# A hybrid attention, expert and recurrent block on one Trainium2 core: input and output laid out by channels, the last residual split between two engines, and blank matmuls moved around the first two expert inputs

## The chip, the cores and the metric

The program runs on one core of a Trainium2 chip. The metric is device time in microseconds (us): 404.32 for the kernel before, the median of 3 runs (403.74 to 404.45). TensorE is called PE here (its weight loads PEld), VectorE DVE, ScalarE ACT, GpSimd POOL and SyncE SP. SP and ACT issue the transfers.

## The reference, cut to what matters

Two images of 16 x 16 positions with 64 channels go through a chain of residual blocks: windowed attention with a gate, a norm, full attention, dilated attention over tokens, a mixture of 8 experts, a causal attention, and a recurrence over the 256 tokens. The last two residuals and the end read:

```python
t = t + _L2_ffn_ref(_ln_t(t), ...)        # gate, top 2 of 8 experts, GELU between two products
t = t + _L3_attn_ref(_ln_t(t), ...)
t = t + _L3_ffn_ref(_ln_t(t), ...)        # the recurrence
...
def step(carry, xs):                       # once for each of 256 tokens
    h, c = carry
    i_t = jax.nn.sigmoid(xi_t + h @ V_i)
    g_t = jnp.tanh(xg_t + h @ V_c)
    o_t = jax.nn.sigmoid(xo_t + h @ V_o)
    c_new = h * c + i_t * g_t
    h_new = o_t * jnp.tanh(c_new)
    return ((h_new, c_new), h_new)
```

A step needs the `h` and `c` of the step before, so the 256 steps run one after the other.

## The kernel before

Everything is held on chip with the two images times 64 channels on the 128 partitions and the 256 tokens along the free axis. Each engine has its own list of instructions, written out by hand in program order; semaphores (`on("name")`) link them, and an engine waits in order. Nothing reorders the work.

**The start.** SP loads `x` token by token (`xtm`, L209: 128 tokens on the partitions, 64 channels in a row, so pieces of 256 bytes), then the constants `cst` and the rest. ACT issues the first weights `w0s` and the vectors `vcs`. PE runs 9 blank matmuls (`keep_clock`, L417, operands zero) and then turns `xtm` into `xf` (channels on the partitions) with two transposes (L425) and one more blank; DVE copies the result out (L783). Then come the products with the weights for keys (L430), queries (L431) and the gate (L432), and DVE makes the masked keys `km` (L792), which the first scores (L459) wait for. DVE takes the smallest score of a row at L813, which also reads the position table `rel`.

**The experts.** After the third norm, PE makes the gate's logits (L643), then `up(0)` and `up(1)`, the first products of two experts (L652), then 8 blank matmuls, then `up(2)`, which first waits for the GELU of expert 0 on ACT (L370) and has one blank matmul of its own. DVE works out the experts' weights meanwhile. From `up(2)` on, PE goes through `up`, `down` (L668) and the spreading of weights (L661) without a gap. ACT makes one `exp` for the gate, changes its function table and then runs the GELUs in order. POOL adds the experts' results (`t3part`, L256).

**The recurrence.** A loop over 16 bodies of 16 steps (PE L748, ACT, DVE L1031, each with its own copy). In a step PE adds the products with the two parts of h, `ha` and `hb` (L740), ACT makes the gates (L394, L396, L400) and the tanh (L406), and DVE makes `ha` (L1039), `hb` (L1042), the cell (L1045), `hs` (L1047) and `hc` (L1049). SP and POOL have nothing to do in it.

**The end.** When `hs` is complete, DVE adds `t4` in two halves (L1052), PE turns each half back to tokens (L769), DVE copies each out of PSUM (L1055), and SP stores each with a transfer of its own (L218).

Of the kernel before, what the change touches and what calls it, by code (L numbers as in the profile page):

```python
# [33 lines left out]
UP_FIRST = 5  # L34
PADT = 3
CHUNK = 8
STEPS_IN_BODY = 2 * CHUNK
HSCALE = 256.0
VSCALE = 16.0
# [35 lines left out]
def build(nc, x, const, later, vec, positions, w0, w1, w2, w3, w4, w5, out):  # L75
    with ExitStack() as ctx:
        def sb(name, shape, dt=F32):
            return ctx.enter_context(nc.sbuf_tensor(name, shape, dt))
# [3 lines left out]
        def on(name):  # L82

            if name not in semaphores:
                semaphores[name] = ctx.enter_context(nc.semaphore("s_" + name))
            return semaphores[name]
# [2 lines left out]
        bank = [banks[i // 2][:, i % 2] for i in range(8)]  # L89


        xtm = sb("xtm", [P, HALVES, B, C])
        cst, ltr = sb("cst", [P, width(CONST)]), sb("ltr", [P, width(LATER)])
        vcs = sb("vcs", [P, width(VECS)])
        w0s, w1s, w2s = sb("w0s", [P, width(W0)]), sb("w1s", [P, width(W1)]), sb("w2s", [P, width(W2)])
# [8 lines left out]
        def v(name):  # L104
            return cols(vcs, VECS, name)
# [80 lines left out]
        ha, hb = sb("ha", [P, 1], F16), sb("hb", [P, 1], F16)  # L186
        hs = sb("hs", [P, N + STEPS_IN_BODY])
        ysum = sb("ysum", [P, N])
        ytm = sb("ytm", [P, HALVES, B, C])

        ident = c("ident")

# [13 lines left out]
        @block.sync  # L206
        def _(sp):
            for b in range(B):
                sp.dma_start(xtm[:, :, b], x[b].rearrange("(h p) c -> p h c", h=HALVES)).then_inc(on("x_in"), 16)  # L209
            sp.dma_start(cst[:], const).then_inc(on("const_in"), 16)  # L210
            for pair in range(HEADS // 2):
                sp.dma_start(rel[:, pair], positions[:, pair]).then_inc(on("rel_in%d" % pair), 16)
            for w, name, dram in ((ltr, "later_in", later), (w1s, "w1_in", w1), (w2s, "w2_in", w2), (w3s, "w3_in", w3),
                                  (w5s, "w5_in", w5), (w4s, "w4_in", w4)):
                sp.dma_start(w[:], dram).then_inc(on(name), 16)
            for h in range(HALVES):
                sp.wait_ge(on("y_tm"), h + 1)
                sp.dma_start(out[:, h * P:(h + 1) * P, :].rearrange("b p c -> p b c"), ytm[:, h]).then_inc(on("out"), 16)  # L218
            sp.wait_ge(on("out"), 16 * HALVES)

        @block.gpsimd
        def _(pool):
            pool.memset(epsc[:, 0:1], 1e-5).then_inc(on("eps_set"), 1)
            pool.memset(epsc[:, 1:2], 1e-3).then_inc(on("eps_set"), 1)
            pool.memset(blank[:], 0.0).then_inc(on("blank_set"), 1)  # L225
            pool.memset(vch[:], 0.0).then_inc(on("vch_zero"), 1)
            pool.memset(kp[:], 0.0).then_inc(on("kpad_zero"), 1)
            pool.memset(vp[:], 0.0).then_inc(on("vpad_zero"), 1)
            pool.memset(x5[:], 0.0).then_inc(on("x5_zero"), 1)
            pool.memset(ones[:], 1.0).then_inc(on("ones_set"), 1)  # L230

            pool.wait_ge(on("of0"), 1)
            pool.wait_ge(on("const_in"), 16)
            pool.tensor_copy(idb[:], ident).then_inc(on("idb_ready"), 1)
            pool.wait_ge(on("later_in"), 16)
            pool.tensor_copy(oneh[:], c("onehot")[0:PARTS]).then_inc(on("oneh_ready"), 1)

            pool.wait_ge(on("w5_in"), 16)
            vw = w5s[:, 3 * P:6 * P]
            flat = vparts[:].rearrange("p a g m -> p a (g m)")  # L240
            for part in (slice(0, 3 * P), slice(6 * P, 9 * P)):
                pool.tensor_scalar(w5s[:, part], w5s[:, part], PRE, None, ALU.mult).then_inc(on("ub_scaled"), 1)
            pool.tensor_scalar(vsc[:], vw, VSCALE, None, ALU.mult).then_inc(on("v_split"), 1)
            pool.wait_ge(on("v_split"), 1)
            pool.tensor_copy(flat[:, 0], vsc[:]).then_inc(on("v_split"), 1)
            pool.wait_ge(on("v_split"), 2)
            pool.tensor_tensor(vrest[:], vsc[:], flat[:, 0], ALU.subtract).then_inc(on("v_split"), 1)
            pool.wait_ge(on("v_split"), 3)
            pool.tensor_copy(flat[:, 1], vrest[:]).then_inc(on("v_parts"), 1)

            pool.wait_ge(on("t2"), HALVES)
            for e in range(E):
                pool.wait_ge(on("weighted"), e + 1 + (e == E - 1))
                if e:
                    pool.wait_ge(on("t3_part"), e)
                pool.tensor_tensor(t3part[:, e], t3part[:, e - 1] if e else t2[:], ye[:, e], ALU.add)\  # L256
                    .then_inc(on("t3_part"), 1)

        @block.scalar
        def _(act):  # L260
# [149 lines left out]
        def _(pe):  # L410
            mm = pe.matmul

            def keep_clock(free_bank, n):


                for _ in range(n):
                    mm(free_bank[:], blank[:, 0:P], blank[:], start=True, stop=True, skip_group_check=True)  # L417
# [1 line left out]

            pe.wait_ge(on("blank_set"), 1)  # L420
            keep_clock(bank[1], WARM_UP)
            pe.wait_ge(on("const_in"), 16)
            pe.wait_ge(on("x_in"), 16 * HALVES)
            for h in range(HALVES):
                pe.transpose(bank[7][:, h * P:(h + 1) * P], xtm[:, h].rearrange("p b c -> p (b c)"), ident)\  # L425
                  .then_inc(on("x_turned"), 1)
            keep_clock(bank[1], 1)
            pe.wait_ge(on("xf"), 1)
            pe.wait_ge(on("w0_in"), 16)
            mm(bank[5][:, 0:N], cols(w0s, W0, "k"), xf[:], start=True, stop=True).then_inc(on("k0_mm"), 1)  # L430
            mm(bank[0][:, 0:N], cols(w0s, W0, "q"), xf[:], start=True, stop=True).then_inc(on("q0_mm"), 1)  # L431
# [214 lines left out]
            def up(e):  # L646
                if e >= 2:
                    pe.wait_ge(on("gelu"), e - 1)
                    keep_clock(up_pair[e % 2][:, 0], 1)
                for b in range(B):  # L650
                    r = slice(b * C, (b + 1) * C)
                    m = mm(up_pair[e % 2][:, b, 0:N], cols(w3s, W3, "up")[r, e * HID:(e + 1) * HID], x3[r, :],  # L652
                           start=True, stop=True)
                m.then_inc(on("up_mm"), 1)
# [10 lines left out]
            def down(e):  # L665
# [3 lines left out]
                           hg[:, e, b * N:(b + 1) * N], start=True, stop=True, skip_group_check=True)  # L669
                m.then_inc(on("down_mm"), 1)  # L670

            up(0)
            up(1)
            keep_clock(bank[3], 8)
            up(2)
            down(0)
            pe.wait_ge(on("cw_parts"), 2)
# [70 lines left out]
            with pe.Fori(0, N, STEPS_IN_BODY) as base:  # L748
                for u in range(STEPS_IN_BODY):
# [14 lines left out]
                        b_part(1 - parity, at)  # L764
                    elif at < 6:
                        x_part(1 - parity, at - 3, base + (parity + 1) * CHUNK)
            for h in range(HALVES):
                pe.wait_ge(on("ysum"), h + 1)
                pe.transpose(bank[h][:, 0:P], ysum[:, h * P:(h + 1) * P], ident).then_inc(on("y_turned"), 1)  # L769

        @block.vector
        def _(dve):
# [6 lines left out]
                ins.then_inc(on("dve_link"), 1)  # L779
                dve.wait_ge(on("dve_link"), links[0])  # L780

            dve.wait_ge(on("x_turned"), HALVES)
            dve.tensor_copy(xf[:], bank[7][:, 0:N]).then_inc(on("xf"), 1)  # L783
            dve.wait_ge(on("vec_in"), 16)
            ts(bq0s[:], v("bq0"), HD ** -0.5, None, ALU.mult).then_inc(on("bq0s"), 1)
            ts(g2bh[:], v("g2b"), 0.5, None, ALU.mult).then_inc(on("g2bh"), 1)

# [243 lines left out]
            with dve.Fori(0, N, STEPS_IN_BODY) as base, nc.allow_low_precision(reason=split):  # L1031
                for u in range(STEPS_IN_BODY):
                    t, two = base + u, u % 2
                    o = go[:, two, 0:1]
                    dve.wait_ge(on("o_gate"), t + 1)
                    ts(go[:, two, 3:4], o, -1.0, None, ALU.mult).then_inc(on("minus_o"), 1)  # L1036

                    dve.wait_ge(on("tanh_c"), t + 1)
                    dve.tensor_tensor_reduce(terms_a[:, two], tq[:, 0:3], go[:, two, 0:3], HSCALE, 0.0,  # L1039
                                             ALU.mult, ALU.add, ha[:]).then_inc(on("ha_ready"), 1)  # L1040
                    dve.wait_ge(on("minus_o"), t + 1)
                    dve.tensor_tensor_reduce(terms_b[:, two], tq, go[:, two], -HSCALE, 0.0,  # L1042
                                             ALU.mult, ALU.add, hb[:]).then_inc(on("hb_ready"), 1)

                    stt(out=cell[:], in0=gt, scalar=gi[:], in1=hc[:], op0=ALU.mult, op1=ALU.add)\  # L1045
                        .then_inc(on("cell_ready"), 1)
                    tt(hs[:, bass.ds(t, 1)], tc, o, ALU.mult).then_inc(on("h_ready"), 1)  # L1047
                    dve.wait_ge(on("h_ready"), t + 1)
                    tt(hc[:], hs[:, bass.ds(t, 1)], cell[:], ALU.mult).then_inc(on("hc_ready"), 1)  # L1049
            dve.wait_ge(on("h_ready"), N)  # L1050
            for h in half:
                tt(ysum[:, h], hs[:, h], t4[:, h], ALU.add).then_inc(on("ysum"), 1)  # L1052
            for h in range(HALVES):
                dve.wait_ge(on("y_turned"), h + 1)
                dve.tensor_copy(ytm[:, h].rearrange("p b c -> p (b c)"), bank[h][:, 0:P]).then_inc(on("y_tm"), 1)  # L1055


def constants(np):
# [120 lines left out]
```

## Time and profile before

| | us |
|---|---|
| median of 3 runs | 404.32 (403.74 to 404.45) |
| the profiled execution | 405.37 |
| its span, first to last instruction | 403.6 |
| PE busy | 280.4 (69%) |
| DVE busy | 256.0 (63%) |
| ACT busy | 212.6 (53%) |
| POOL busy | 16.9 (4%) |

The span is 1.8 us shorter than the profiled execution, and that execution is 1.05 us above the median of the runs. Busy shares say little here: no engine is full, because in the recurrence each waits for another once a step. Times inside the span are counted from its start.

### The profile page before, as it was taken

To read this page: it belongs to the slowest core of one execution; us is meant where nothing else is said; L and a number is where in the kernel's file an instruction comes from. 1 tells how busy PE (TensorE), PEld (TensorE's weight loads), DVE (VectorE), ACT (ScalarE), POOL (GpSimd) and SP (SyncE) were. 2 spreads that over 40 slices of the span, in tenths; PEclk is the share of its full clock that TensorE was granted. 3 is DMA by queue.
4 is the path that set the end of the run, shared out by engine and by line. 5 is a ranking of instruction groups with operands and counts; after the bars stand their busy time and mean duration, and the time that the engine had idled before them with its cause. 6 is when DMAs were issued, how large, how long until landed. Compare 5 with 4: busy or idle time off the path is not lost.

```text
span 403.6 us, 12076 instructions
## 1 busy us (share of the span) xinstructions
PE 280.4 (69%) x3372; PEld 219.2 (54%) x3372; DVE 256.0 (63%) x2320; ACT 212.6 (53%) x1182; POOL 16.9 (4%) x28
## 2 busy tenths in 40 slices
PE   8898899999666666666666566666666656566663
PEld 3564466447555555555555555555555555555553
DVE  2885557555566666666666666666666666666665
ACT  2996552546554554554554554554555555555552
POOL 4006000032000000000000000000000000000000
PEclk9999999899555555555555555555555555555555
DMA  7600000000000000000000000000000000000000
GB/s 269 261 4 0 2 0 2 0 2 0 3 2 0 0 0 0 0 0 0 0 0 0 0 0 0 0 0 0 0 0 0 0 0 0 0 0 0 0 0 13
DMA packets 2973, 5.64 MB, mean 14 GB/s; under 512 B 1424, under 2 KB 1680, under 8 KB 2960
## 3 DMA queue, kind: packets, MB, share of 16 engines
q1 hardware_dynamic: 2672, 5.11, 3.4%
q10 hardware_dynamic: 288, 0.37, 0.3%
q8 instruction: 7, 0.11, 0.1%
q14 instruction: 6, 0.05, 0.0%
HBM read 5.34 MB, written 0.13 MB: 14 GB/s over the span
## 4 chain that ended last, share of the span: by engine, by line
ACT 39%; PE 36%; DVE 15%; issue 10%; POOL 0%; DVEq 0%; ACTq 0%; POOLq 0%
ACT banks L406 21%; PE banks L740 18%; ACT gi L394 11%; DVE ha L1039 6%; DVE terms_a L1039 5%; ACT banks L396 5%; PE banks L417 4%; PE banks L471 1%; PE banks L652 1%; PE banks L459 1%; PE banks L668 1%; PE banks L486 1%; PE banks L537 1%; DVE sc L813 1%; PE banks L627 1%
## 5 line engine op out<-in xcount | busy, mean ns | idle before, releaser
L740 PE MATMUL banks<-ha,vparts 128*128 128x1 f16 x1536 | 95.7, 169 | 110.6 <-DVE ha L1039 110.6
L740 PEld LDWEIGHTS banks<-ha,vparts 128*128 128x128 f16 x1536 | 74.9, 107 | 133.5 <-DVE ha L1039 133.5
L394 ACT ACTIVATE gi<-banks 128x1 f32<-128x1 f32 x256 | 43.8, 171 | 144.7 <-PE banks L740 144.7
L406 ACT ACTIVATE banks<-banks,hc,gi 128x2 f32<-128x2 f32 x256 | 83.6, 326 | 0.0
L1036 DVE TENSOR_SCALAR go<-go 128x1 f32<-128x1 f32 x256 | 39.4, 154 | 65.9 <-ACT go L400 65.9
L740 PE MATMUL banks<-hb,vparts 128*128 128x1 f16 x768 | 76.5, 165 | 0.0
L740 PEld LDWEIGHTS banks<-hb,vparts 128*128 128x128 f16 x768 | 60.6, 104 | 0.0
L1039 DVE CUSTOM_DVE_ANT_0 terms_a<-banks,go 128x3 f32<-128x3 f32 x256 | 41.1, 161 | 29.3 <-ACT banks L406 0.2
L736 PE MATMUL banks<-x,w5s 128*128 (+1 forms) x198 | 56.0, 358 | 0.2 <-DVE x L862 0.2
L514 PE MATMUL banks<-ones,w5s 128*128 128x8 f32 x198 | 55.9, 357 | 0.0
L1045 DVE SCALAR_TENSOR_TENSOR cell<-banks,gi,hc 128x1 f32<-128x1 f32 x256 | 54.8, 214 | 0.0
L736 PEld LDWEIGHTS banks<-x,w5s 128*128 128x128 f32 x198 | 49.0, 308 | 0.4 <-DVE x L862 0.4
L514 PEld LDWEIGHTS banks<-ones,w5s 128*128 128x128 f32 x198 | 49.1, 308 | 0.1
L400 ACT ACTIVATE go<-banks 128x3 f32<-128x3 f32 x256 | 48.4, 189 | 0.0
L1049 DVE TENSOR_TENSOR hc<-hs,cell 128x1 f32<-128x1 f32 x256 | 40.6, 159 | 8.8
L396 ACT ACTIVATE banks<-banks 128x1 f32<-128x1 f32 x256 | 42.8, 167 | 0.0
L1042 DVE CUSTOM_DVE_ANT_0 terms_b<-banks,go 128x4 f32<-128x4 f32 x256 | 40.0, 156 | 0.0
L1047 DVE TENSOR_TENSOR hs<-banks,go 128x1 f32 x256 | 38.0, 149 | 0.0
L417 PE MATMUL banks<-blank 128*128 128x512 bf16 x84 | 27.1, 427 | 1.4 <-POOL blank L225 1.4
L1042 DVE DVE_READ_ACCUMULATOR2_ANT hb<- 128x1 f16 x256 | 21.9, 85 | 0.0
L1039 DVE DVE_READ_ACCUMULATOR2_ANT ha<- 128x1 f16 x256 | 21.8, 85 | 0.0
L287 ACT ACTIVATE pr<-sc,nmx 128x176 f32<-128x176 f32 x32 | 13.8, 433 | 2.4 <-DVE nmx L813 2.3
(219 smaller groups left out, 275.7 us busy)
## 6 DMA issues: line engine op xcount, KB each, us to landing
rel<-in_positions SPq DMA_DIRECT2D x4, 352.0 KB, 6.6
w3s<-in_w SPq DMA_DIRECT2D x1, 776.0 KB, 10.7
ltr<-in_later SPq DMA_DIRECT2D x1, 756.0 KB, 8.6
w2s<-in_w SPq DMA_DIRECT2D x1, 640.0 KB, 9.6
w5s<-in_w SPq DMA_DIRECT2D x1, 576.0 KB, 11.4
w0s<-in_w ACTq DMA_DIRECT2D x1, 336.0 KB, 3.9
w1s<-in_w SPq DMA_DIRECT2D x1, 256.0 KB, 8.8
w4s<-in_w SPq DMA_DIRECT2D x1, 192.0 KB, 11.4
```

Of the source, the lines that this page charges most:

```text
L394: act.activation(gi[:], bank[pre + 1][:, at:at + 1], ACT.Sigmoid, scale=1.0 / PRE)
L396: act.activation(gt, bank[pre][:, at:at + 1], ACT.Tanh, scale=1.0 / PRE)\
L400: act.activation(go[:, two, 0:3], bank[pre + 2][:, at:at + 1].broadcast_to([P, 3]), ACT.Sigmoid, scale=1.0 / PRE).then_inc(on("o_gate"), 1)
L406: act.activation(tc_ends, gt.broadcast_to([P, 2]), ACT.Tanh, scale=gi[:], bias=hc[:]).then_inc(on("tanh_c"), 1)
L417: mm(free_bank[:], blank[:, 0:P], blank[:], start=True, stop=True, skip_group_check=True)
L514: return mm(bank[3 * parity + k][:, 0:CHUNK], w5s[:, (6 + k) * P:(7 + k) * P], ones[:], start=True, stop=False, skip_group_check=True)
L736: return mm(bank[3 * parity + k][:, 0:CHUNK], w5s[:, k * P:(k + 1) * P], x5[:, bass.ds(start, CHUNK)], start=False, stop=False, skip_group ...
L740: return mm(bank[3 * parity + k][:, at:at + 1], vparts[:, part, k], h, start=False, stop=False, skip_group_check=True)
L1039: dve.tensor_tensor_reduce(terms_a[:, two], tq[:, 0:3], go[:, two, 0:3], HSCALE, 0.0, ALU.mult, ALU.add, ha[:]).then_inc(on("ha_ready"), 1)
L1042: dve.tensor_tensor_reduce(terms_b[:, two], tq, go[:, two], -HSCALE, 0.0, ALU.mult, ALU.add, hb[:]).then_inc(on("hb_ready"), 1)
L1045: stt(out=cell[:], in0=gt, scalar=gi[:], in1=hc[:], op0=ALU.mult, op1=ALU.add)\
L1049: tt(hc[:], hs[:, bass.ds(t, 1)], cell[:], ALU.mult).then_inc(on("hc_ready"), 1)
```

## The change

1. The host passes `x` with channels on the partitions, so SP loads `xf` at once (two transfers, 64 partitions with 256 elements in a row each). The two transposes, the blank matmul behind them and DVE's copy are gone; PE waits for `x_in` and `w0_in` alone. DVE waits for `x_in`, `vec_in` and `const_in` at its start.
2. The output leaves as `(128, 256)`, channels on the partitions, and the host turns it. PE's two transposes and DVE's two copies at the end are gone.
3. POOL adds `hs` and `t4` for the first 224 tokens as soon as step 224 is done; SP stores these. DVE adds the last 32 after the loop and SP stores them.
4. In front of `up(0)` and between `up(0)` and `up(1)` stand 2 blank matmuls each, and 3 in place of 8 stand behind `up(1)`.

```diff
-                sp.dma_start(xtm[:, :, b], x[b].rearrange("(h p) c -> p h c", h=HALVES)).then_inc(on("x_in"), 16)
+                sp.dma_start(xf[b * C:(b + 1) * C], x[b * C:(b + 1) * C]).then_inc(on("x_in"), 16)
...
-            for h in range(HALVES):
-                sp.wait_ge(on("y_tm"), h + 1)
-                sp.dma_start(out[:, h * P:(h + 1) * P, :].rearrange("b p c -> p b c"), ytm[:, h]).then_inc(on("out"), 16)
-            sp.wait_ge(on("out"), 16 * HALVES)
+            for part, made in zip(stored, ("ysum_most", "ysum_last")):
+                sp.wait_ge(on(made), 1)
+                sp.dma_start(out[:, part], ysum[:, part]).then_inc(on("out"), 16)
+            sp.wait_ge(on("out"), 16 * len(stored))
...
+            most = stored[0]
+            pool.wait_ge(on("h_ready"), N - LAST)
+            pool.wait_ge(on("t4"), HALVES)
+            pool.tensor_tensor(ysum[:, most], hs[:, most], t4[:, most], ALU.add).then_inc(on("ysum_most"), 1)
...
             keep_clock(bank[1], WARM_UP)
-            pe.wait_ge(on("const_in"), 16)
-            pe.wait_ge(on("x_in"), 16 * HALVES)
-            for h in range(HALVES):
-                pe.transpose(bank[7][:, h * P:(h + 1) * P], xtm[:, h].rearrange("p b c -> p (b c)"), ident)\
-                  .then_inc(on("x_turned"), 1)
-            keep_clock(bank[1], 1)
-            pe.wait_ge(on("xf"), 1)
+            pe.wait_ge(on("x_in"), 16 * B)
             pe.wait_ge(on("w0_in"), 16)
...
+            keep_clock(bank[3], 2)
             up(0)
+            keep_clock(bank[3], 2)
             up(1)
-            keep_clock(bank[3], 8)
+            keep_clock(bank[3], 3)
             up(2)
...
-            for h in range(HALVES):
-                pe.wait_ge(on("ysum"), h + 1)
-                pe.transpose(bank[h][:, 0:P], ysum[:, h * P:(h + 1) * P], ident).then_inc(on("y_turned"), 1)
...
-            dve.wait_ge(on("x_turned"), HALVES)
-            dve.tensor_copy(xf[:], bank[7][:, 0:N]).then_inc(on("xf"), 1)
+            dve.wait_ge(on("x_in"), 16 * B)
             dve.wait_ge(on("vec_in"), 16)
+            dve.wait_ge(on("const_in"), 16)
...
+            last = stored[1]
             dve.wait_ge(on("h_ready"), N)
-            for h in half:
-                tt(ysum[:, h], hs[:, h], t4[:, h], ALU.add).then_inc(on("ysum"), 1)
-            for h in range(HALVES):
-                dve.wait_ge(on("y_turned"), h + 1)
-                dve.tensor_copy(ytm[:, h].rearrange("p b c -> p (b c)"), bank[h][:, 0:P]).then_inc(on("y_tm"), 1)
+            tt(ysum[:, last], hs[:, last], t4[:, last], ALU.add).then_inc(on("ysum_last"), 1)
```

**PE at the experts.** `x` here is the normed input, `w3s` the experts' weights, L643 the gate's logits, L652 `up`, L668 `down`. Before:

```order
L643 MATMUL banks<-w3s,x 128x16 x2
L652 MATMUL banks<-x,w3s 128x256 x4
L417 MATMUL banks<-blank 128x512 x9
L652 MATMUL banks<-x,w3s 128x256 x2
L668 MATMUL banks<-hg,w3s 64x256 x2
```

The same place in the changed kernel, where the gate's logits are L642, `up` is L651, `down` L667 and a blank L422:

```order
L642 MATMUL banks<-w3s,x 128x16 x2
L422 MATMUL banks<-blank 128x512 x2
L651 MATMUL banks<-x,w3s 128x256 x2
L422 MATMUL banks<-blank 128x512 x2
L651 MATMUL banks<-x,w3s 128x256 x2
L422 MATMUL banks<-blank 128x512 x4
L651 MATMUL banks<-x,w3s 128x256 x2
L667 MATMUL banks<-hg,w3s 64x256 x2
```

Nine blanks in one piece became 2, 2 and 4, so 8 in all; `up(0)` stands behind two of them.

**PE at the start.** Before, from the first instruction on:

```order
L417 MATMUL banks<-blank 128x512 x9
L425 MATMUL banks<-cst,xtm 128x128 x2
L417 MATMUL banks<-blank 128x512
L430 MATMUL banks<-xf,w0s 128x256
L431 MATMUL banks<-xf,w0s 128x256
```

And now:

```order
L422 MATMUL banks<-blank 128x512 x9
L429 MATMUL banks<-xf,w0s 128x256
L430 MATMUL banks<-xf,w0s 128x256
L431 MATMUL banks<-xf,w0s 32x256
L458 MATMUL banks<-km,q 128x176 x4
```

The keys' product stands directly behind the nine blanks.

**DVE at the end.** `hs` and `hc` of the last step, the loop's branch, and what follows. Before:

```order
L1047 TENSOR_TENSOR hs<-banks,go 128x1
L1049 TENSOR_TENSOR hc<-hs,cell 128x1
L1031 REGISTER_ALU
L1031 COMPARE_AND_BRANCH
L1052 TENSOR_TENSOR ysum<-hs,t 128x128 x2
L1055 COPY ytm<-banks 128x128 x2
```

And now:

```order
L1045 TENSOR_TENSOR hs<-banks,go 128x1
L1047 TENSOR_TENSOR hc<-hs,cell 128x1
L1029 REGISTER_ALU
L1029 COMPARE_AND_BRANCH
L1050 TENSOR_TENSOR ysum<-hs,t 128x32
```

One short add is left behind the loop; the 224 other columns are POOL's.

## Rows read from the trace of the kernel before

**Rows 1.** The page: its span, and the chain that ended last, by line.

```profile
span 403.6 us, 12076 instructions
...
ACT banks L406 21%; PE banks L740 18%; ACT gi L394 11%; DVE ha L1039 6%; DVE terms_a L1039 5%; ACT banks L396 5%; PE banks L417 4%; PE banks L471 1%; PE banks L652 1%; PE banks L459 1%; PE banks L668 1%; PE banks L486 1%; PE banks L537 1%; DVE sc L813 1%; PE banks L627 1%
```

**Rows 2.** The chain in order of time, last steps and end: start us, us, what.

```profile
397.07 0.28 PE banks L740 x4
...
398.23 0.28 PE banks L740 x4
...
399.83 0.30 DVE ysum L1052
...
400.69 0.50 DVE ytm L1055 x2
```

**Rows 3.** The chain at the turn of the loop behind the first body.

```profile
119.11 0.28 PE banks L740 x4
...
121.48 0.30 PE banks L740 x4
```

**Rows 4.** The timeline of the start: start us, us, engine line op.

```profile
0.71 0.45 ACTq L268 DMA_DIRECT2D w0s<-in_w  x1
...
1.35 4.02 PE L417 MATMUL banks<-blank 128*128 128x512 bf16 x9 [1.35 <-POOL blank L225]
...
2.22 1.85 SPq L212 DMA_DIRECT2D rel<-in_positions  x4
...
5.17 0.67 PE L425 MATMUL banks<-cst,xtm 128*128 128x128 f32 x2
...
6.36 0.70 PE L430 MATMUL banks<-xf,w0s 128*128 128x256 f32 x2
...
7.10 0.99 DVE L792 TENSOR_SCALAR km<-banks,vcs,cst 128x256 f32<-128x256 f32 x2 [0.67 <-PE banks L430]
```

**Rows 5.** Transfers of the whole span: KB each, median us from issue to landing.

```profile
w0s<-in_w ACTq DMA_DIRECT2D x1, 336.0 KB, 3.9
...
out_y<-ytm SPq DMA_DIRECT2D x2, 64.0 KB, 1.7
```

**Rows 6.** Transfers whose issue falls between 2.6 and 3.0 us.

```profile
rel<-in_positions SPq DMA_DIRECT2D x2, 352.0 KB, 5.9
```

**Rows 7.** PE's timeline at the dilated attention and at the experts.

```profile
62.96 1.24 PE L417 MATMUL banks<-blank 128*128 128x512 bf16 x5
...
74.14 1.66 PE L652 MATMUL banks<-x,w3s 64*128 64x256 f32 x8
75.73 3.23 PE L417 MATMUL banks<-blank 128*128 128x512 bf16 x9
78.89 0.70 PE L652 MATMUL banks<-x,w3s 64*128 64x256 f32 x4
```

**Rows 8.** Stretches at the experts: busy us of each engine, then granted clock.

```profile
74.00:74.50 0.50, 0.50 (x6) 0.45 (x8) 0.22 (x2) 0.00 (x0) 0.00 (x0) 1.00 0.00 0
74.50:75.00 0.50, 0.50 (x6) 0.42 (x4) 0.43 (x3) 0.08 (x1) 0.00 (x0) 0.61 0.00 0
...
78.00:78.50 0.50, 0.50 (x4) 0.20 (x2) 0.00 (x0) 0.00 (x0) 0.00 (x0) 0.98 0.00 0
```

**Rows 9.** The timeline at the experts: ACT's first two GELUs.

```profile
76.46 1.27 ACT L370 ACTIVATE hg<-banks,vcs 128x512 f32<-128x512 f32 x2
```

**Rows 10.** The timeline of the end: SP's two stores.

```profile
401.01 0.91 SPq L218 DMA_DIRECT2D out_y<-ytm  x2
```

**Rows 11.** POOL's groups by form (busy us, mean ns), for its adds.

```profile
L256 POOL TENSOR_TENSOR t3part<-t3part,ye 128x256 f32<-128x256 f32 x7 | 5.1, 726 | 2.2 <-DVE ye L1003 1.5
```

**Rows 12.** Timeline from 35.8 us: POOL's casts, and DVE adding two SBUF tiles.

```profile
35.88 0.50 POOL L245 CAST vparts<-vsc 128x384 f16<-128x384 f32 x1
...
37.38 0.29 DVE L844 TENSOR_TENSOR y<-pg,xf 128x128 f32<-128x128 f32 x1
37.45 0.58 POOL L249 CAST vparts<-vrest 128x384 f16<-128x384 f32 x1
```

More of the change, by code:

```diff
@@ L36 @@
 CHUNK = 8
+LAST = 32
 STEPS_IN_BODY = 2 * CHUNK
@@ L89, in build @@
         bank = [banks[i // 2][:, i % 2] for i in range(8)]
-        xtm = sb("xtm", [P, HALVES, B, C])
         cst, ltr = sb("cst", [P, width(CONST)]), sb("ltr", [P, width(LATER)])
@@ L188, in build @@
         ysum = sb("ysum", [P, N])
-        ytm = sb("ytm", [P, HALVES, B, C])
+        stored = (slice(0, N - LAST), slice(N - LAST, N))
         ident = c("ident")
@@ L1155 @@
     parts["const"], parts["later"] = constants(np)
-    parts["x"] = np.ascontiguousarray(a["x"].reshape(B, N, C))
+    parts["x"] = np.ascontiguousarray(a["x"].reshape(B, N, C).transpose(0, 2, 1)).reshape(P, N)
     rpb = np.pad(L0["rpb"], ((0, 0), (APAD, APAD), (BPAD, BPAD)))
@@ L1174 @@
             for n in order]
-    args.append(nc.dram_tensor("out_y", (B, N, C), F32, kind="ExternalOutput").ap())
+    args.append(nc.dram_tensor("out_y", (P, N), F32, kind="ExternalOutput").ap())
     build(nc, *args)
     r = run(nc, [{f"in_{n}": parts[n] for n in order}], core_ids=[0])
-    return r.results[0]["out_y"].reshape(B, SIDE, SIDE, C)
+    return np.ascontiguousarray(r.results[0]["out_y"].reshape(B, C, N).transpose(0, 2, 1)).reshape(B, SIDE, SIDE, C)
```

## The prediction

> **What bounds the kernel now.** I read the page first, then the chain of waits in order of time, then the timeline, stretch by stretch, at the three places that the change touches. The page's chain [rows 1] is held by the recurrence: L406, L740, L394, L1039 and L396 are its lines. In order of time its step is 398.23 - 397.07 = 1.16 us [rows 2], and 256 of them are 297 us of a span of 403.6 [rows 1]. Every step is the same ring PE, ACT, DVE, PE, with no engine full. The change adds nothing to the ring, so it can win only in front of it and behind it, and it can lose in it if something disturbs 256 steps. At the turn of the loop two steps take 121.48 - 119.11 = 2.37 in place of 2.32 [rows 3]: 0.05 a turn, 0.8 for 16.
>
> Outside the ring three stretches matter. At the start the reader is to see nine blanks from 1.35 on and L425 behind them at 5.17, which means that PE was free at 5.17 and that x and the constants were there; the keys' product L430 starts only at 6.36, after the turn and the copy [rows 4]. At the experts `up(0)` and `up(1)` run from 74.14, then nine blanks from 75.73, and `up(2)` at 78.89 [rows 7]. At the end DVE's first add starts at 399.83, its copies at 400.69 [rows 2], SP's two issues at 401.01 [rows 10].
>
> **The start.** Two transposes, a blank and the copy leave. What is left to wait for at 5.17 is the weights: issued at 0.71 [rows 4], landed 3.9 later [rows 5], at 4.6. The vectors are issued right behind them; DVE's two small instructions on them now run before the keys' product is there, and so beside PE. L430 can thus start at 5.17 in place of 6.36: 1.19 at most. But the blanks up to there are (5.17 - 1.35) / 9 = 0.42 us apart, where five blanks at 62.96 take 1.24 with the last one's end [rows 7], some 0.22 apart: PE is still at 1.2 GHz at 5.17. From L430's start to `km` it took 7.10 - 6.36 = 0.74 [rows 4] at 2.4 GHz. At 1.2 GHz its two passes take longer: nothing more if the clock rises just then, the double (1.48) if all of it is stretched. Only the columns are stretched, and a pass of 256 single-precision columns is worth about one blank, so I take 0.74 + 2 x 0.21 = 1.16: `km` starts at 6.33, and the gain is **0.8** (between 0.45 and 1.19). Next in line is the second table of positions: the first is issued at 2.22, four in 1.85 [rows 4], the first two land 5.9 after issue by the median [rows 6], the second so at 2.7 + 5.9 = 8.6 or somewhat later. `km` takes 0.99 [rows 4] and I give the scores as long, so the first minimum can start at 8.3 and needs the second table half a microsecond later: just hidden; if not, a few tenths of the gain are lost, which the lower bound holds.
>
> **The experts.** Here the clock decides. The granted clock is 1.00 until 74.5, 0.61 in the next half microsecond, and 0.98 from 78.0 on [rows 8]: PE fell to 1.2 GHz at about 74.6, behind the small products of the norm and of the gate, and got 2.4 GHz back at 78.0. So most of the nine blanks were run at half speed. What `up(2)` has to wait for is the first GELU. Two of them take 1.27 from 76.46 on [rows 9], so the first ends at 77.1; a blank (0.22) and its issue (0.1) behind it give 77.45, and `up(2)` started at 78.89. PE works without a gap from `up(2)` on, so what is won there is won for good, up to **1.4**. In the new order, if the clock holds: two blanks 74.14 to 74.57, `up(0)` (0.64 by the one at 78.89 [rows 7]) to 75.2, two blanks to 75.6, `up(1)` to 76.3, three blanks to 76.9; PE then waits for the GELU, and the full 1.4 is there. `up(0)` comes 0.43 later than before, which costs nothing: the GELU starts at 76.46, behind the exp and ACT's table change, and finds it done. If the clock falls at 74.6 all the same: `up(0)` to 75.5, blanks to 76.3, `up(1)` to 77.2, three blanks to 78.3, `up(2)` at 78.6, a gain of 0.3. I take 1.4: the stretch before the fall is the one that now has two dense blanks in place of products on 64 of the 128 rows. That this is enough is what I know least.
>
> **The end.** Before: second issue at 401.01 + 0.46 = 401.47 [rows 10], landed 1.7 later [rows 5] at 403.17, and 0.43 to the end of the span. After: the add of 32 columns starts at the same point behind `hs` and takes less than the 0.30 of 128 columns [rows 2]; I take 0.2. SP issues at 400.05, the store lands at 401.75 if it takes the 1.7 of a four times larger one, end at 402.2: **1.4** (1.3 with the add at 0.30; up to 1.7 if a small store lands sooner, of which no row speaks). The large store has 32 steps (37 us) to land.
>
> **POOL in the ring.** Its add of 224 columns costs 0.726 x 224 / 256 = 0.64 [rows 11], once, 37 us before it is needed. On the ring it costs something only if it holds DVE up. Two rows bear on this: DVE added two SBUF tiles at 37.38 in its usual 0.29, beside a cast on POOL that took 0.58 where the same shape took 0.50 [rows 12]. By that POOL gives way, and by less than 0.1. The upper bound is the whole 0.64, if `hc` stands behind the add. I take 0.1. The Trainium skill (SBUF — State Buffer, Who interferes with whom) says that a DVE instruction with two SBUF inputs and a GpSimd one that reads SBUF exclude each other for a whole instruction, whichever starts first; `hc` is such an instruction. By it the sum would be up to half a microsecond worse; the cast's 0.08 agrees with some exclusion, but no row here shows DVE as the loser.
>
> **The sum.** 0.8 + 1.4 + 1.4 - 0.1 = 3.5. The profiled execution (405.37, span 403.6) would become 401.9 with a span of 400.1. That execution is 1.05 above the median of the runs, so part of what I remove, the fall of the clock above all, may be rarer in them; I take the sum from the median, 404.32 - 3.5 = **400.8**.
>
> **The rivals.**
> - *The clock falls among the ups all the same* (0.17): gain 0.3 there, 404.32 - 2.4 = 401.9. For it: the fall stands only 0.5 us behind the first new blank, so most of what precedes it is unchanged. Against it: the new order also keeps blanks between the ups.
> - *The timed runs of before did not lose the clock there* (0.15): nine blanks then end at 74.14 + 1.28 + 1.94 = 77.4, when the GELU allows `up(2)` anyway, and the middle edit gives nothing: 404.32 - 2.1 = 402.2. For it: the profiled execution's 1.05 over the median. Against it: a profile may lengthen an execution by itself.
> - *POOL's add takes DVE's SBUF access in the ring* (0.08): `hc` waits for up to 0.64, some of which the turn of the loop hides (step 224 ends a body): 401.3. It is the skill's rule above, made a place: the first `hc` behind step 224.
> - *The loop gets slower* (0.04): all four copies of its body stand elsewhere in their programs now, and the turn, 0.05 late today [rows 3], may not stay hidden. With 0.3 more a turn, 16 x 0.3 = 4.8, it is 405.6, slower than before; it decides from 0.22 a turn on (3.5 / 16). Nothing in the trace speaks for it but that the turn is not free now.
> - *The change does not do what it says*: for the two ends I see no way, since nothing else is on the path there (0.02: 403.5 to 405).
>
> What is left for the forecast is 0.54. Its own range is 400.2 to 401.3.
>
> **How the numbers follow.** The best case takes the upper bounds: 1.19 + 1.4 + 1.7 = 4.3, 400.0. The range leaves out the loop, the void case and the far ends of the others: 400.0 to 402.3. A measurement of this kernel can tell about 0.2% (0.8 us) from no change. All cases but the last two gain 2 us or more: faster 0.93, within 0.2% 0.04, slower 0.03.
>
> **What would show it.** Start: the keys' product directly behind the ninth blank at 5.2, `km` at 6.3. Experts: granted clock 1.00 from 74 to 78 less the shift of the start, and `up(2)` 0.3 behind the end of the first GELU. End: one store behind the add, 2.2 us from the add's end to the end of the span. Ring: 297.7 us from first to last product, with no step over 1.3 near step 224. Wrong would make it: a clock that rises later at the start, blanks that do not hold it at the experts, a longer turn, or a 128-byte-a-row store that lands later than the 256-byte one.

## The result, and the profile after

The changed kernel takes 401.91 us (median of 6 runs, 401.2 to 402.13) beside 404.12 for the one before (6 runs, 403.74 to 405.46). The ratio is 0.9939, with a 95% interval of 0.9923 to 0.9955: 2.2 to 2.5 us faster. The forecast was 400.8 with a range of 400.0 to 402.3. Sign and range hold; the point is 1.1 too low. The forecast had taken its 3.5 from a median of 404.32, and the median of before is now 404.12, so of the gain itself 1.3 is missing (3.5 forecast, 2.2 measured). The larger part of this study is about that.

The profiled execution of the changed kernel is its fastest, 401.2 with a span of 399.4; that of before was among its slowest, 405.37 with 403.6. The two profiles differ by 4.2 us, the medians by 2.2. So the profiles must not be subtracted from each other without asking whether each is typical.

**The start.** The timeline of the changed kernel (start us, us, engine line op, what ended the wait), which answers to [rows 4]:

```profile
1.35 3.51 PE L422 MATMUL banks<-blank 128*128 128x512 bf16 x9 [1.35 <-POOL blank L225]
...
1.95 0.58 SPq L210 DMA_DIRECT2D cst<-in_const  x1
...
4.70 0.59 PE L429 MATMUL banks<-xf,w0s 128*128 128x256 f32 x2
...
5.84 0.15 DVE L783 TENSOR_SCALAR bq0s<-vcs 128x1 f32<-128x1 f32 x1 [5.84 <-DMA cst<-in_const]
...
5.98 0.98 DVE L790 TENSOR_SCALAR km<-banks,vcs,cst 128x256 f32<-128x256 f32 x2
```

And its chain of waits there:

```profile
1.95 3.75 DMA cst<-in_const
```

The masked keys start at 5.98 in place of 7.10. Two things differ from the forecast. Nine blanks took 3.51 where they had taken 4.02: the clock rose before the last of them, and the keys' product took 0.59 and ended at 5.29, where I had reckoned 1.16 from its start to the masked keys. And it did not matter, since DVE sat until 5.84 for the constants. Their transfer is issued 0.23 later than before, at 1.95, because the two transfers of x in its new form take SP 1.18 to issue where the old ones took 0.95. (At the start the clock is read from the blanks, 0.43 apart at 1.2 GHz and 0.22 at 2.4; the profile's column for it reads 1.00 there in every run.)

**The experts.** PE's timeline, answering to [rows 7], and two stretches with the granted clock behind POOL's column, answering to [rows 8]:

```profile
72.94 0.59 PE L422 MATMUL banks<-blank 128*128 128x512 bf16 x2
73.46 0.70 PE L651 MATMUL banks<-x,w3s 64*128 64x256 f32 x4
74.09 0.61 PE L422 MATMUL banks<-blank 128*128 128x512 bf16 x2
74.63 0.70 PE L651 MATMUL banks<-x,w3s 64*128 64x256 f32 x4
75.27 1.21 PE L422 MATMUL banks<-blank 128*128 128x512 bf16 x4
76.40 0.70 PE L651 MATMUL banks<-x,w3s 64*128 64x256 f32 x4
```

```profile
70.00:75.00 5.00, 4.54 (x33) 2.63 (x32) 3.09 (x23) 3.46 (x7) 0.00 (x0) 1.00 0.00 0
75.00:80.00 5.00, 5.00 (x30) 1.72 (x26) 2.04 (x11) 2.97 (x5) 0.00 (x0) 1.00 0.00 0
```

The clock held, and `up(2)` stands at 76.40 where it stood at 78.89: 2.49 earlier, 1.12 of it from the start and 1.37 from this stretch. Against this one profile of before, the forecast's 1.4 is exact.

**The ring and GpSimd's add.** The timeline at step 224:

```profile
359.69 0.24 PE L741 MATMUL banks<-ha,vparts 128*128 128x1 f16 x3 [0.76 <-DVE ha L1037]
...
359.94 0.16 DVE L1047 TENSOR_TENSOR hc<-hs,cell 128x1 f32<-128x1 f32 x1
359.99 0.66 POOL L262 TENSOR_TENSOR ysum<-hs,t 128x224 f32<-128x224 f32 x1 [269.11 <-DVE hs L1045]
...
360.90 0.24 PE L741 MATMUL banks<-ha,vparts 128*128 128x1 f16 x3 [0.37 <-DVE ha L1037]
```

POOL starts 0.05 behind the start of `hc`; the step takes 1.21, which is what it takes at any turn of the loop [rows 3].

**The end.** The changed kernel's last product and its add, from the chain; SP's issue, from the timeline; the landing, from the transfers (KB, us). They answer to [rows 2, 5, 10]:

```profile
395.74 0.28 PE banks L741 x4
...
397.33 0.19 DVE ysum L1050
```

```profile
397.56 0.34 SPq L218 DMA_DIRECT2D out_y<-ysum  x1
```

```profile
out_y<-ysum SPq DMA_DIRECT2D x1, 16.0 KB, 1.5
```

From the last step's first product to the end of the span it is now 399.4 - 395.74 = 3.66, and was 403.6 - 398.23 = 5.37: 1.71 won, 0.3 more than forecast. The issue comes 0.23 behind the add's start as reckoned; the store of 16 KB lands after 1.5, not 1.7, and what follows the landing is 0.34, not 0.43.

### The profile page after: what moved, and what is told of

Read it like the earlier page. It is cut to its first block, busy times and chain, and to the rows that moved or that the text cites. A ratio compares the mean times of both kernels' runs of the same rounds, so it can differ in the third digit from the quotient of the medians.

```text
span 399.4 us, 12062 instructions
## 1 busy us (share of the span) xinstructions
PE 276.7 (69%) x3366; PEld 217.6 (54%) x3366; DVE 254.8 (64%) x2316; ACT 212.3 (53%) x1182; POOL 17.6 (4%) x29
## 4 chain that ended last, share of the span: by engine, by line
ACT 39%; PE 35%; DVE 15%; issue 10%; DMA 1%; SPq 0%; DVEq 0%; ACTq 0%
ACT banks L411 21%; PE banks L741 18%; ACT gi L399 11%; DVE ha L1037 6%; DVE terms_a L1037 5%; ACT banks L401 5%; PE banks L422 3%; PE banks L470 1%; PE banks L651 1%; PE banks L458 1%; PE banks L667 1%; DMA cst<-in_const 1%; PE banks L485 1%; PE banks L536 1%; DVE sc L811 1%
## 5 line engine op out<-in xcount | busy, mean ns | idle before, releaser
L422 PE MATMUL banks<-blank 128*128 128x512 bf16 x82 | 25.1, 401 | 1.4 <-POOL blank L225 1.4
```

## The experiments

Two theories of the missing gain were set against each other. **A**: the fall of the clock at the experts, on which the 1.4 rests, is rare; the timed runs of before did not have it. **B**: it is there in every run, and start and end give less than the trace says. For the start, **C** says that the constants' landing sets it, **D** that PE's clock does. The experiments were timed in three groups, each with runs of the kernel before beside it, and a gain is taken from those: 404.16 (30 runs) for experiments 1 to 4, 403.85 (11) for 5 to 8, 403.90 (11) for 9 to 12. The mean clock of an execution is its granted TensorE clock over the whole span, where 1 is 2.4 GHz and 0.5 is 1.2.

**1. The kernel before, again** (no edit).

> The kernel before, unchanged, for the span and the mean granted clock of each execution. Theory A (the fall of the clock at the experts happens in a few executions only): spans between 402 and 403.7, most at 402.1 to 402.6, and those at 403 and above with the lower mean clock. Theory B (it falls in every execution): all spans within 0.4 of 403.6, mean clock 0.62 in each.

Measured: 404.27, ratio 1.0006 (0.9995 to 1.0017). Of the 30 before runs in this group, 22 are at 403.8 to 404.5 with mean clocks of 0.624 to 0.629, and eight at 405.35 and above. Only two of these eight have the 0.622 of the case's profiled execution. PE's timeline at the experts in this profile (span 402.5):

```profile
75.48 2.38 PE L417 MATMUL banks<-blank 128*128 128x512 bf16 x9
77.80 0.70 PE L652 MATMUL banks<-x,w3s 64*128 64x256 f32 x4
```

And the granted clock in that place, behind POOL's column:

```profile
76.00:77.00 1.00, 1.00 (x6) 0.41 (x5) 0.83 (x5) 0.99 (x2) 0.00 (x0) 1.00 0.00 0
```

Nine blanks take 2.38 with the last one's end, in place of 3.23 [rows 7]: 2.4 GHz all through. `up(2)` starts 3.38 behind the first up (74.42), where it was 4.75. That is A. The profiles of experiments 3, 4 and 7, which have the old order of blanks too, also show 1.00 from 70 to 80: of five profiles with that order, the case's own is the only one with the fall. The other half of A's expectation fell: the other six long runs have a mean clock of 0.626 or 0.627, no lower than the rest. That does not prove that they kept the clock at the experts, for the mean is a weak sign. In every profile with blanks at the ups the clock also falls for good as the recurrence begins, at 99.8 in the changed kernel's and at 103.4 in experiment 8's; these 3.6 us move the mean by 0.0045 (3.6 x 0.5 / 400), as much as the fall at the experts does in 3.4.

**2. The moved blanks alone**, on the kernel before.

```diff
+            keep_clock(bank[3], 2)
             up(0)
+            keep_clock(bank[3], 2)
             up(1)
-            keep_clock(bank[3], 8)
+            keep_clock(bank[3], 3)
```

> Before with the blanks around the first two ups moved, nothing else. Theory A: the median stands 0 to 0.5 below before (403.6 to 404.1), since most executions had nothing to win there. Theory B: 1.4 below (402.7).

Measured: 404.21 (12 runs), ratio 0.9998 (0.998 to 1.0015). PE's timeline:

```profile
76.50 1.21 PE L417 MATMUL banks<-blank 128*128 128x512 bf16 x4
77.64 0.70 PE L652 MATMUL banks<-x,w3s 64*128 64x256 f32 x4
```

The edit is worth nothing measurable: the interval reaches from 0.8 faster to 0.6 slower, and 1.4 is outside it. `up(2)` stands at 77.64, beside 77.80 in experiment 1, and most of that 0.16 came from the start (scores at 8.37 in place of 8.51). With the clock up, both orders end in the same wait for the first GELU. Three of the 12 runs took 405.5: the long executions are there with either order.

**3. Start and end without the moved blanks**: the changed kernel with edit 2 undone.

> The changed kernel with the old order of blanks (none before the ups, 8 behind): start and end of the change alone. Theory A: nearly all of the timed gain, 401.9 to 402.3. Theory B: 1.4 above the changed kernel, 403.3, because the ends would be worth only 0.8 to 1.1 in timed runs.

Measured: 401.79 (7 runs), ratio 0.9956 (0.9939 to 0.9973). All of the timed gain is here, and B is out.

**4. The start alone**, on the kernel before: x by channels, no turns, no copy.

> Before with x loaded by channels and no turns at the start, nothing else. Theory A: 0.4 to 1.1 below before, by where the clock rises in each execution; the masked keys start at 5.9 to 6.4 and wait for the constants (landing at 5.8), not for PE, where the clock rises early. Theory B (the start is worth nothing in timed runs since the constants come late): within 0.2 of before.

Measured: 403.20 (12 runs), 0.96 below before, ratio 0.9985 (0.9969 to 1.0001), so the median and the ratio do not say quite the same; its runs go from 402.75 to 405.30. From the chain:

```profile
1.95 3.83 DMA cst<-in_const
...
6.13 1.00 DVE km L785 x2
```

The masked keys start 1.0 to 1.2 earlier than before (7.10 in the case's profile, 7.37 in experiment 1's). The chain has them wait for the constants, but PE's keys' product, 0.92 from 5.17 on, ends at 6.09, at nearly the same time. In experiment 3 the same transfer landed later still, and the keys followed:

```profile
1.95 4.36 DMA cst<-in_const
...
6.67 0.92 DVE km L788 x2
```

**5. One transfer of x in place of two**, on the changed kernel, which brings the constants' issue from 1.95 to 1.15.

```diff
-            for b in range(B):
-                sp.dma_start(xf[b * C:(b + 1) * C], x[b * C:(b + 1) * C]).then_inc(on("x_in"), 16)
+            sp.dma_start(xf[:], x).then_inc(on("x_in"), 16)
```

> The changed kernel with x loaded by one transfer of 128 partitions in place of two of 64, so that the constants are issued about 0.6 earlier. Theory C (the start is now set by the landing of the constants, at 5.8 to 6.4): the masked keys start 0.3 to 0.6 earlier, and the median is 401.4 to 401.6. Theory D (the start is set by PE's clock, as forecast): no change, 401.9.

**6. The constants ahead of x**: as 5, with the two lines exchanged.

> As one_x, but the constants are issued before x. Theory C: the constants are there by 4.6, the masked keys then wait for PE's product and start at 5.5 (clock up early) to 6.3 (late), and the median is 401.1 to 401.5. Theory D: no change, 401.9.

Measured: 401.51 and 401.46, ratios 0.9941 (0.9929 to 0.9954) and 0.9940 (0.9927 to 0.9953), 2.3 to 2.4 below before where the changed kernel is 2.2 below: no difference that can be told. The timeline of 5:

```profile
1.15 0.42 SPq L209 DMA_DIRECT2D cst<-in_const  x1
...
5.16 1.06 PE L428 MATMUL banks<-xf,w0s 128*128 128x256 f32 x2
...
6.26 0.99 DVE L789 TENSOR_SCALAR km<-banks,vcs,cst 128x256 f32<-128x256 f32 x2 [1.06 <-PE banks L428]
```

And that of 6, where the constants land at 3.9 (issued at 0.72, landed 3.2 later):

```profile
6.27 0.99 DVE L789 TENSOR_SCALAR km<-banks,vcs,cst 128x256 f32<-128x256 f32 x2 [1.21 <-PE banks L428]
```

The constants no longer hold DVE, and it now waits 1.06 or 1.21 for PE, whose keys' product at 1.2 GHz takes 1.06 in place of 0.59. The masked keys are no earlier than in the changed kernel (5.98, and 6.27 in experiment 9). So C and D are both half right: two gates stand at nearly the same time, the constants at 5.8 to 6.8, and PE's product at about 5.3 (4.70 + 0.59, clock up early) to 6.2 (5.16 + 1.06, late), and taking one away leaves the other. (A third is close behind: in experiment 8 PE's product itself waited for x until 5.0.)

**7. The end alone**, on the kernel before.

> Before with the new end alone (channels in the output, GpSimd's add of 224 columns, two stores). Both theories have 1.4 to 1.7 below before by the trace: 402.5 to 402.8. If start and end add up, head_only's gain of 0.6 to 1.0 and this one make the 2.2 to 2.5 of the whole change; if the end gives 2.2 alone, the start is worth nothing in it.

Measured: 402.28 (6 runs), 1.57 below before, ratio 0.9966 (0.9954 to 0.9979). With the start's 0.96 that is 2.5 for the two parts, and 2.2 to 2.4 for them together (changed kernel, experiment 3). Read the other way, experiment 3's 2.37 less this 1.57 leaves 0.8 for the start.

**8. 55 more adds on GpSimd** in the ring, on the changed kernel, one behind every fourth step and each over 256 columns; they go to a scratch tile and no output depends on them.

```diff
+            for n in range(4, N - LAST, 4):
+                pool.wait_ge(on("h_ready"), n)
...
+                pool.tensor_tensor(scratch[:], t4[:], t4[:], ALU.add).then_inc(on("scratched"), 1)
             pool.wait_ge(on("h_ready"), N - LAST)
```

> The changed kernel with 55 more adds of 256 columns on GpSimd (t4 + t4 into a scratch tile, behind every fourth step), which change no output. If GpSimd's add takes DVE's access to SBUF in the ring, each costs up to 0.5, in all 5 to 27: 407 to 429. If GpSimd gives way, or the slack around hc hides it, 401.9 to 403.

Measured: 402.13 (5 runs), ratio 0.9954 (0.9941 to 0.9967). In its profile the constants came later than in any other (4.70 from issue, by the chain), so what it stands above the others need not be the adds. POOL's group, and the timeline in the middle of a body:

```profile
L266 POOL TENSOR_TENSOR scratch<-t 128x256 f32<-128x256 f32 x55 | 33.6, 611 | 231.4 <-DVE hs L1051 231.4
```

```profile
150.14 0.24 PE L747 MATMUL banks<-ha,vparts 128*128 128x1 f16 x3 [0.32 <-DVE ha L1043]
...
151.30 0.24 PE L747 MATMUL banks<-ha,vparts 128*128 128x1 f16 x3 [0.32 <-DVE ha L1043]
...
151.55 0.16 DVE L1053 TENSOR_TENSOR hc<-hs,cell 128x1 f32<-128x1 f32 x1
151.59 0.61 POOL L266 TENSOR_TENSOR scratch<-t 128x256 f32<-128x256 f32 x1 [4.03 <-DVE hs L1051]
```

33.6 us of adds beside the ring cost it nothing: from the first step's product (100.15) to the last one's (396.66) it is 296.5, as in the changed kernel and before. `hc` starts 0.04 to 0.05 ahead of POOL in 54 of the 55 (0.11 in the first), and the next `hc` comes 1.16 later, when the add of 0.61 is over.

**9. The changed kernel, again** (no edit).

> The changed kernel, unchanged, beside the three below: 401.7 to 402.1, with single executions from 401.2 on, where the clock rises early and the constants land early.

Measured: 401.72 (401.51 to 402.07), ratio 0.9946 (0.9933 to 0.9958). Here the clock was still low at the keys' product. The constants were there at 6.10, and the masked keys came behind the product, at 6.27:

```profile
5.17 1.06 PE L429 MATMUL banks<-xf,w0s 128*128 128x256 f32 x2
...
6.10 0.15 DVE L783 TENSOR_SCALAR bq0s<-vcs 128x1 f32<-128x1 f32 x1 [6.10 <-DMA cst<-in_const]
...
6.27 0.99 DVE L790 TENSOR_SCALAR km<-banks,vcs,cst 128x256 f32<-128x256 f32 x2
```

**10. One transfer of x, and seven blanks at the start.**

```diff
-WARM_UP = 9
+WARM_UP = 7
```

> The changed kernel with x in one transfer and 7 blanks at the start in place of 9. Theory C: with the constants out of the way, the ninth blank's end (5.17) is the next to set the start; PE can begin at 4.3, the masked keys at 5.1 to 5.6, and the median is 0.6 to 1.0 below the changed kernel in this call (400.9 to 401.3). Rival: fewer blanks let the clock rise later or fall, and nothing or less than nothing is won.

Measured: 401.03 (5 runs, 400.64 to 401.55), ratio 0.9925 (0.9912 to 0.9937): 2.9 below before and 0.7 below experiment 9, which is the changed kernel timed in the same group. It has the lowest median here. Experiment 5, the same kernel with nine blanks, was 2.3 below its own before; the intervals of the two ratios overlap, so the 0.5 that the two blanks seem to be worth rests on the profiles as much as on the times. The timeline:

```profile
1.35 3.17 PE L421 MATMUL banks<-blank 128*128 128x512 bf16 x7 [1.35 <-POOL blank L224]
...
4.61 1.19 PE L428 MATMUL banks<-xf,w0s 128*128 128x256 f32 x2
...
5.84 0.99 DVE L789 TENSOR_SCALAR km<-banks,vcs,cst 128x256 f32<-128x256 f32 x2 [0.47 <-PE banks L428]
```

PE gets to the keys' product at 4.61 in place of 5.16 (experiment 5), and the masked keys start at 5.84 in place of 6.26. My expectation had the total right (0.6 to 1.0 below) and both places too early (4.3, and 5.1 to 5.6). The first weights, issued at 0.71, land 3.8 later, at 4.5, just as the seventh blank ends, so still fewer blanks have little left to give. Product and blank run at the same low clock here, so a blank that delays the product is a loss.

**11. No GpSimd part**: DVE adds all 256 columns behind the loop, one store.

```diff
-            for part, made in zip(stored, ("ysum_most", "ysum_last")):
-                sp.wait_ge(on(made), 1)
-                sp.dma_start(out[:, part], ysum[:, part]).then_inc(on("out"), 16)
+            sp.wait_ge(on("ysum_last"), 1)
+            sp.dma_start(out, ysum[:]).then_inc(on("out"), 16)
...
-            tt(ysum[:, last], hs[:, last], t4[:, last], ALU.add).then_inc(on("ysum_last"), 1)
+            tt(ysum[:], hs[:, 0:N], t4[:], ALU.add).then_inc(on("ysum_last"), 1)
```

> The changed kernel without GpSimd's part: DVE adds all 256 columns after the loop, one store of 128 KB. The add is 0.3 longer by its columns, the store 0.1 to 0.3 longer than that of 16 KB: 0.3 to 0.6 above the changed kernel. If the split of the add is what pays at the end, more than 1.

Measured: 402.24 (402.17 to 402.46), ratio 0.9958 (0.9945 to 0.9971), 0.52 above experiment 9. The timeline and the store:

```profile
397.85 0.42 DVE L1045 TENSOR_TENSOR ysum<-hs,t 128x256 f32<-128x256 f32 x1
398.31 0.35 SPq L217 DMA_DIRECT2D out_y<-ysum  x1
```

```profile
out_y<-ysum SPq DMA_DIRECT2D x1, 128.0 KB, 1.7
```

The add is 0.23 longer and the store 0.2: that is most of the 0.5. The split is a third of the end's gain of 1.57; the rest is the turns and copies that are gone.

**12. No blanks around the first two ups**, on the changed kernel (the one that `up(2)` has itself stays).

> The changed kernel with no blanks around the first two ups but the one that up(2) has itself. If the blanks hold the clock in most executions, it falls here and the products behind run at half speed for a while: 0.5 to 1.7 above the changed kernel. If they do nothing, the same time, as up(2) waits for the first GELU in any case.

Measured: of 7 executions four took 410.5 to 411.0 with mean clocks of 0.607 to 0.610, and three 401.7 to 402.8 with 0.622 to 0.629; the median is 410.48. PE's timeline and some stretches of the profiled one (410.51):

```profile
76.60 0.61 PE L422 MATMUL banks<-blank 128*128 128x512 bf16 x1 [1.93 <-ACT hg L375]
77.14 1.23 PE L651 MATMUL banks<-x,w3s 64*128 64x256 f32 x4
```

```profile
80.00:85.00 5.00, 5.00 (x18) 1.82 (x19) 0.75 (x2) 0.92 (x2) 0.00 (x0) 0.50 0.00 0
85.00:90.00 5.00, 5.00 (x18) 1.25 (x14) 1.85 (x4) 1.15 (x2) 1.44 (x2) 0.50 0.00 0
...
95.00:100.00 5.00, 4.86 (x35) 3.56 (x32) 2.30 (x7) 2.28 (x5) 2.90 (x4) 0.83 0.00 0
```

```profile
76.00:77.00 1.00, 0.40 (x1) 0.10 (x1) 0.86 (x6) 1.00 (x2) 0.00 (x0) 0.63 0.00 0
...
96.00:97.00 1.00, 1.00 (x8) 0.30 (x4) 1.00 (x3) 0.80 (x2) 0.71 (x1) 0.63 0.00 0
```

PE is idle for 1.93 in front of `up(2)`, falls to 1.2 GHz in the microsecond from 76 on and is busy without a gap at that clock until between 96 and 97. My expectation (0.5 to 1.7) missed the size: I had the clock come back after some 3 us, as in [rows 8], where dense blanks ran. With the experts' products and one blank for each expert it stayed low for the whole stretch. The same order kept the clock in the fastest executions; which way an execution goes no run here explains. The order of before, with its eight blanks behind the two ups, never took this long in 88 executions.

## Why the prediction was right, and where it was off

- **The ring is untouched**: right. First to last step is 296.5 us before (101.69 to 398.23) and after (99.20 to 395.74). The 297.7 that I gave as its sign was miscounted: from the first to the last of 256 products there are 255 steps and 15 turns of the loop, 255 x 1.16 + 15 x 0.05 = 296.6.
- **The experts, 1.4**: this term fails. It was exact against the profiled execution of before and is zero against the timed runs (experiment 2: 0.9998). The step that failed is in the sum: "I take the sum from the median", with all of a term whose cause, the fall of the clock, was seen in a single execution. The rival "the timed runs of before did not lose the clock there", priced at 402.2 with a chance of 0.15, is what happened; it measured 401.91. The warning was in hand: the profiled execution stood 1.05 above the median, and the fall alone, priced at 1.4, was enough to explain that. That the point came within 1.1 although 1.4 of its 3.5 was not there is in part luck: 0.2 of it is the lower median of before, and the start, the end and the ring were each booked 0.1 to 0.2 too low, by the experiments with one part alone.
- **The start, 0.8**: right in size (0.96 of medians in experiment 4, whose interval just reaches no change; 0.8 from experiments 3 and 7; 1.12 by the profiles), half wrong in its reason. I had made PE's clock the gate and had let the constants be "there" because they were at 5.17 in the old kernel. They were issued later in the new one, and a wait on them was added to DVE, which I named and did not price. I also read 0.74 from the product's start to the masked keys as a time at 2.4 GHz: that product took 0.70 [rows 4], and 0.59 with the clock up (changed kernel), so a part of it ran at 1.2 GHz. The 1.16 that I made of it for the low clock was near all the same: it is 1.10 in experiments 5, 6 and 9. The bounds (0.45 to 1.19) hold.
- **The end, 1.4**: 1.57 by medians, 1.71 by the profiles. The missing part is the small store, 1.5 in place of the 1.7 of a larger one, for which I had no row.
- **GpSimd in the ring, 0.1**: zero. The rival that made it a place is out by experiment 8. The rule of the Trainium skill (SBUF — State Buffer, Who interferes with whom) has the two exclude each other, and by it `hc`, which starts first, would go on and POOL would be the one that waits. No run here shows DVE waiting. None shows POOL waiting either: its adds start 0.04 to 0.05 behind the start of an `hc` of 0.16, so the two overlap in the records. An add that starts first and meets an `hc` was not tried.
- **The clock falls all the same, the slower loop, no effect**: none was seen in the 11 runs of the changed kernel.

What stays open: some executions of before (6 of 30) and of experiments 1, 2, 3 and 7 are 1.2 to 2.3 longer than the median of their kernel at a mean clock of 0.626 or 0.627. Experiment 2 has three of them, so the old order of blanks is not their cause; no profile shows one. How often the old order loses the clock at the experts is open too. Of 88 executions with the old order in the three groups four have a mean clock of 0.622 or less (two of before, two of experiment 4), and none of 42 with the new one (experiments 2, 5, 6, 8 to 11). But all four fell in the first group, 4 of 60 there, where the new order had only 12 executions; in the other two groups the old order had none in 28 either. So it is not shown that the moved blanks take anything away. If they do, it is an execution in twenty that is 1.4 longer, and nothing in a median. What experiment 12 shows is that to have no blanks there is costly.

## What to carry to other kernels

Before a stretch at a low clock is booked as a gain, hold the profiled execution against the median and run the old kernel again: a term seen once belongs in the sum with the share of runs that have it. When a step is taken out, list everything that the next instruction waits for with the time at which each is there in the new order of issues, since a second gate may stand within half a microsecond, as here, and then sets what is won. Blanks in a wait that exists anyway cost nothing here (in experiment 12 two of the executions that kept the clock without them took 401.7 and 402.0, as those with them do), and without them the clock was lost in four of seven executions, in a fifth perhaps for a shorter time (402.8, mean clock 0.622); blanks in front of work that was ready delayed it (experiment 10).

## What the hardware showed that I had not expected

- The clock at the start rises at a different time in executions of one program: nine blanks took 3.51 in one and 4.02 in others, and the keys' product behind them 0.59 to 1.06. In the changed kernel the masked keys started at 5.98 in the one and at 6.27 in another.
- PE fully busy with the experts' products did not get 2.4 GHz back for about 20 us once it had lost it (experiment 12), at a cost of 8.8 (410.48 against 401.72); with nine blanks in the stretch it was back in 3.4 [rows 8]. One trace shows each.
- Two transfers of x, to 64 partitions each, kept SP's queue for 1.18 together, where the two by tokens had kept it for 0.95 and one to 128 partitions keeps it for 0.38 (experiment 5).
